# Adding the attention bias on VectorE and subtracting the maximum on GpSimd

## The reference

```
tokens  = patches(x, 16 long, step 8) @ W + b             # 64 x 93 x 128
h = tokens
xn = layernorm(layernorm(h)) * gamma + beta
q, k, v = conv3(wq1 @ xn), conv3(wk1 @ xn), conv3(wv1 @ xn)   # 8 heads of 64
sim = q k^T / 8 - |i - j| * slope_h                       # 93 x 93 for each head
sim = where(j > i, -max, sim)
h = h + (softmax(sim) @ v) @ wout^T
h = h + experts(layernorm(h))   # top 2 of 16, each expert's mean hidden row
```

## Time and profile before

| what | value |
|---|---|
| median of 3 runs | 845.18 us (844.15 to 845.42) |
| the profiled execution: its own time | 846.1 us |
| the profiled execution: its span | 844.4 us |
| PE busy | 752.6 us (89%) |
| DVE busy | 615.9 us (73%) |
| ACT busy | 468.9 us (56%) |
| POOL busy | 383.3 us (45%) |

### The profile page before, as it was taken

The page is one execution under the profiler, slowest core; times in us unless marked ns, Lnnn a source line. Parts: engine busy times, 40 slices in busy tenths (PEclk is TensorE's granted clock), DMA queues, the critical chain, the costliest instruction groups (busy, mean ns, idle before and its releaser), DMA issues. The chain is left out here.

```text
span 844.4 us, 20971 instructions
## 1 busy us (share of the span) xinstructions
PE 752.6 (89%) x6670; PEld 696.4 (82%) x6670; DVE 615.9 (73%) x1621; ACT 468.9 (56%) x1021; POOL 383.3 (45%) x408
## 2 busy tenths in 40 slices
PE   5577999999999999999999999999786318999987
PEld 5466999999999999999999999977675208999983
DVE  2145778888888888888888888899573145888865
ACT  3345566656566665656666566555333107899950
POOL 3442243666556565555656556545241552222200
PEclk9787999999999999999999999999898658999989
DMA  6321123332112112111212211050000022222205
GB/s 190 99 72 46 47 72 117 102 104 64 48 47 66 47 47 65 50 46 46 68 46 50 65 48 48 19 208 20 10 15 6 19 69 73 64 62 62 62 17 145
DMA packets 42246, 53.89 MB, mean 64 GB/s; under 512 B 13651, under 2 KB 28947, under 8 KB 41680
## 3 DMA queue, kind: packets, MB, share of 16 engines
q1 hardware_dynamic: 26304, 37.13, 15.5%
q0 software_dynamic: 13120, 14.05, 6.0%
q10 hardware_dynamic: 2768, 2.00, 0.8%
HBM read 42.69 MB, written 10.26 MB: 63 GB/s over the span
## 5 line engine op out<-in xcount | busy, mean ns | idle before, releaser
L1106 POOL DMA_INDIRECT expert_rows<-hn,slot x128 | 167.7, 1310 | 92.5 <-DVE slot L951 59.9
L1043 POOL TENSOR_TENSOR x_lo<-x_raw,x_hi 128x752 fp32r<-128x752 f32 x64 | 114.9, 1795 | 151.7 <-ACT x_hi L667 151.7
L831 DVE SCALAR_TENSOR_TENSOR qkv<-ps,taps,qkv 128x368 f32<-128x368 f32 x192 | 114.0, 594 | 86.2 <-ACT qkv L675 84.6
L675 ACT ACTIVATE qkv<-ps,taps 128x372 f32<-128x372 f32 x192 | 108.6, 567 | 90.1 <-PE ps L408 89.8
L834 DVE SCALAR_TENSOR_TENSOR qkv<-ps,taps,qkv 128x364 f32<-128x364 f32 x192 | 114.6, 597 | 6.8
L406 PE MATMUL ps<-x_hi,wtok_hi 128*128 128x376 f32 x256 | 95.3, 372 | 11.3 <-DVE wtok_lo L811 9.0
L500 PEld LDWEIGHTS psO<-vrow,probT 93*93 93x93 f32 x1024 | 93.5, 162 | 4.7 <-ACT probT L700 3.2
L500 PE MATMUL psO<-vrow,probT 93*93 93x65 f32 x1024 | 93.9, 245 | 2.0 <-ACT probT L700 1.1
L407 PE MATMUL ps<-x_lo,wtok_hi 128*128 128x376 f32 x256 | 89.1, 348 | 0.0
L408 PE MATMUL ps<-x_hi,wtok_lo 128*128 128x376 f32 x256 | 89.0, 348 | 0.0
L576 PE MATMUL psO<-wout,attnT 128*93 128x128 f32 x512 | 70.6, 283 | 18.6 <-ACT attnT L746 15.8
(11 more groups left out here) (160 smaller groups left out, 1620.7 us busy)
## 6 DMA issues: line engine op xcount, KB each, us to landing
x_raw<-in_x SPq DMA_DIRECT2D x64, 376.0 KB, 3.2
w1s<-in_w POOLq DMA_DIRECT2D x8, 512.0 KB, 4.9
w<-in_w SPq DMA_DIRECT2D x4, 1024.0 KB, 10.3
xs<-expert_rows SPq DMA_DIRECT2D x54, 64.0 KB, 1.8
xs<-expert_rows POOLq DMA_DIRECT2D x54, 64.0 KB, 2.1
out<-resid SPq DMA_DIRECT2D x16, 160.0 KB, 2.4
expert_rows<-hn,slot POOLq DMA_INDIRECT x128, 3.5
qkv<-in_w_tok ACTq DMA_DIRECT2D x4, 256.0 KB, 6.7
```

The costliest lines, as they stand in the source:

```text
L675: nc.scalar.activation(qkv[u][:, k, :, :], psP[(k + 1) % 2][:, 0:GT].rearrange("p (b n) -> p b n", n=NT), ACT.Copy, scale=taps[:, k, 2:3]) ...
L831: nc.vector.scalar_tensor_tensor(dst[:, :, 1:NT], src[:, :, 0:NT - 1], taps[:, k, 1:2], dst[:, :, 1:NT], ALU.mult, ALU.add).then_inc(tap1_ ...
L1043: nc.gpsimd.tensor_tensor(x_lo[u][:, 0:PIECE], x_raw[u][:, :], x_hi[u][:, 0:PIECE].bitcast(F32), ALU.subtract)\
L1106: nc.gpsimd.indirect_dma_start(rows, bass.IndirectOffsetOnAxis(slot[1 - u][:, c:c + 1], 0), hn[1 - u][:, c % GB, :], None)\
```

## The change

`bias` stays in fp32 and goes straight from HBM to its own tile; `ident16` and the two casts are gone. TensorE no longer writes the bias into `psS`. VectorE adds `bias` as it takes the scores out of `psS` into one of two `score` tiles, and takes the maximum from there. GpSimd subtracts the maximum in place. TensorE's transposes read `score`.

```diff
-        bias = sb("bias", [NT, 2, GT], BF16)
-        ident16 = sb("ident16", [128, 128], BF16)
+        bias = sb("bias", [NT, 2, GT])
-        shifted = sb("shifted", [NT, 2, 4, NT])
+        score = [sb(f"score{u}", [NT, 2, 4, NT]) for u in range(2)]
...
@@ tensor, step
-                                mm = nc.tensor.transpose(psS[:NT, a, hh * NT:(hh + 1) * NT], shifted[:, a, hh, :],
+                                mm = nc.tensor.transpose(psS[:NT, a, hh * NT:(hh + 1) * NT], score[(s + 1) % 2][:, a, hh, :],
...
                         wait(pe, p_evac, n * 2)
-                        for a in range(2):
-                            nc.tensor.matmul(psS[:NT, a, 0:4 * NT], ident16[:NT, :NT], bias[:, a, :],
-                                             start=True, stop=False, skip_group_check=True)
+                        wait(pe, mask_add, n)
...
-                                                      start=False, stop=True, skip_group_check=True)
+                                                      start=True, stop=True)
@@ vector, step
                         dve.wait_ge(s_mm, n + 1)
-                        nc.vector.tensor_reduce(rmax[:, :, :], heads(psS, NT), AXX, ALU.max).then_inc(max_done, 1)
-                        dve.wait_ge(max_done, n + 1)
-                        wait(dve, p_tr, n * 2)
-                        nc.vector.tensor_tensor(shifted[:, :, :, :], heads(psS, NT),
-                                                rmax[:, :, :].unsqueeze(3).broadcast_to([NT, 2, 4, NT]),
-                                                ALU.subtract).then_inc(shift_done, 1)
+                        wait(dve, p_tr, (n - 1) * 2)
+                        nc.vector.tensor_tensor(score[s % 2][:, :, :, :], heads(psS, NT),
+                                                bias[:, :, :].rearrange("p a (h n) -> p a h n", n=NT),
+                                                ALU.add).then_inc(mask_add, 1)
+                        dve.wait_ge(mask_add, n + 1)
+                        wait(dve, shift_done, n)
+                        nc.vector.tensor_reduce(rmax[:, :, :], score[s % 2][:, :, :, :], AXX, ALU.max).then_inc(max_done, 1)
@@ gpsimd, constants
-                nc.gpsimd.tensor_copy(bias[:, :, :].rearrange("p a n -> p (a n)"), bias32[:, :]).then_inc(bias_cast, 1)
-                nc.gpsimd.tensor_copy(ident16[:, :], ident[:, :]).then_inc(bias_cast, 1)
@@ gpsimd, step, behind xnT_lo and ahead of the spread scatters
+                    if f.attn:
+                        pool.wait_ge(max_done, n + 1)
+                        nc.gpsimd.tensor_tensor(score[s % 2][:, :, :, :], score[s % 2][:, :, :, :],
+                                                rmax[:, :, :].unsqueeze(3).broadcast_to([NT, 2, 4, NT]),
+                                                ALU.subtract).then_inc(shift_done, 1)
```

More of the change, by code:

```diff
@@ L98, in build @@
         early = qkv[1][:].rearrange("p k b n -> p (k b n)")
-        bias32, tri32 = early[:NT, 0:2 * GT], early[:NT, 2 * GT:2 * GT + NT]
+        tri32 = early[:NT, 0:NT]
         early0 = qkv[0][:].rearrange("p k b n -> p (k b n)")
@@ L217, in build @@
             sem("proj_mm"), sem("tap2_done"), sem("tap1_done"), sem("conv_done"))
-        v_tr, v_evac, s_mm, max_done, shift_done = (
-            sem("v_tr"), sem("v_evac"), sem("s_mm"), sem("max_done"), sem("shift_done"))
+        v_tr, v_evac, s_mm, mask_add, max_done, shift_done = (
+            sem("v_tr"), sem("v_evac"), sem("s_mm"), sem("mask_add"), sem("max_done"), sem("shift_done"))
         p_tr, p_evac, pv_mm, den_done, norm_done = (
@@ L383, in _ @@
                 sp.dma_start(dst, src).then_inc(proj_w_in, 16)
-            for dst, src in ((bias32[:, :], c_bias), (tri32[:, :], c_tri)):
+            for dst, src in ((bias[:, :, :].rearrange("p a n -> p (a n)"), c_bias), (tri32[:, :], c_tri)):
                 sp.dma_start(dst, src).then_inc(mask_in, 16)
@@ L512, in step @@
                         if s == 0 and isinstance(t, int) and t == 3:
-                            pe.wait_ge(bias_cast, 4)
+                            pe.wait_ge(bias_cast, 2)
                         wait(pe, p_evac, n * 2)
-                        for a in range(2):
-                            nc.tensor.matmul(psS[:NT, a, 0:4 * NT], ident16[:NT, :NT], bias[:, a, :],
-                                             start=True, stop=False, skip_group_check=True)
+                        wait(pe, mask_add, n)
                         for hh in range(4):
@@ L874, in step @@
                     if f.attn:
+                        if s == 0 and isinstance(t, int) and t == 3:
+                            dve.wait_ge(mask_in, 16 * 2)
                         dve.wait_ge(s_mm, n + 1)
-                        nc.vector.tensor_reduce(rmax[:, :, :], heads(psS, NT), AXX, ALU.max).then_inc(max_done, 1)
-                        dve.wait_ge(max_done, n + 1)
-                        wait(dve, p_tr, n * 2)
-                        nc.vector.tensor_tensor(shifted[:, :, :, :], heads(psS, NT),
-                                                rmax[:, :, :].unsqueeze(3).broadcast_to([NT, 2, 4, NT]),
-                                                ALU.subtract).then_inc(shift_done, 1)
+                        wait(dve, p_tr, (n - 1) * 2)
[5 more added lines that the diff above has]
+                        nc.vector.tensor_reduce(rmax[:, :, :], score[s % 2][:, :, :, :], AXX, ALU.max).then_inc(max_done, 1)
                     if f.gate and s == 3:
@@ L1059, in step @@
                 for s in range(GB):
+                    n = (t - 3) * GB + s
                     if f.scat and not f.norm and s == 0:
```

## The result

| | before | changed |
|---|---|---|
| median of 4 runs | 845.08 us | 871.25 us (870.39 to 872.05) |
| ratio | | 1.0311, 95% interval 1.0293 to 1.0329 |
| span of the profiled execution | 844.4 us | 870.0 us |

The changed kernel is 3.1% slower. The forecast of 877 us has the sign right, and the time lies in its range. The parts of the sum are another matter: four of them came out too large, and 8.3 us have a cause that no part of it named.

A forecast was written before the change was run, and what follows sets the result against it. TensorE's instruction list was taken to bound the main stretch, and cross-engine chains the phase's end. Terms 14.0+1.6+3.6+6.0-0.3+5.3+1.4 = +31.6 us on the 844.4 us span gave 876.0, adjusted to 877 us; range 858 to 899.

The forecast's parts named there:

- s=2: Third batch part of a four-batch group: TensorE's list of 9.15 us outlasts the chain, so -0.41 us.
- the next T comes 4.0 us after the add's start: Add, maximum, GpSimd subtract and three handoffs take 4.0 us until T, the start of TensorE's softmax-dependent transpose (line 452).
- step 16: Emptying pipeline, group step without token work: nothing hides the chain, 36.0 against 32.35 us, +3.6 us.
- +1.08: Net change in us per full group of four batches, over thirteen groups (steps 3 to 15): +14.0 us.
- s=1: Second batch part of a group: chain of 8.65 us against TensorE's list of 8.14, +0.10 us.
- s=3: Last batch part of a group: GpSimd's subtract stands behind its 752- and 372-element subtracts, +1.39 us.
- s=0: First batch part of a group: chain of 9.3 us against TensorE's list of 8.89, no change.
- rival C: Handoffs and VectorE's slack better than read: adds in s=1 and s=0 start 0.4 us earlier; 866 us, chance 0.18.
- Steps 17 and 18: Pipeline's end: eight scatters ahead of GpSimd's subtract delay transposes; first +6.0 and -0.3 us, then +5.3 and +1.4.
- Rival A: GpSimd is quick: its subtract costs 0.81 us like the cast, kernel faster at 842 us; chance 0.06.
- D: Rival: a broadcast operand makes GpSimd's subtract cost up to 2.6 us; 920 us, chance 0.05.
- B: Rival: TensorE's pauses before every s=0 bring 3 us at half clock per group; +20, 897 us, chance 0.13.

The follow-up runs named there:

- e4: Changed kernel with GpSimd subtracting the full 93x744 bias table instead of the broadcast maximum, which is left out of the scores; 882.97 us.
- e8: Changed kernel without VectorE's extra wait before the maximum, and in part 3 GpSimd's subtract of the maximum ahead of the 372-element low half; 857.86 us.
- e3: Changed kernel with the eight scatters of steps 17 and 18 behind GpSimd's subtract instead of ahead of it; 868.88 us.
- e10: Changed kernel without VectorE's extra wait, and with the scatters of steps 17 and 18 spread two to a part behind the subtract; 844.28 us.
- e5: Kernel before with eleven small VectorE memsets ahead of the loop and one already fulfilled wait per batch, giving the changed kernel's code layout; 856.75 us.
- e1: Changed kernel without VectorE's wait, ahead of each maximum, for the subtract of the batch before; 864.36 us.
- e7: Changed kernel without VectorE's extra wait, and with every subtract of the maximum on VectorE instead of GpSimd; 862.27 us.
- e2: Kernel before with one already fulfilled VectorE wait per batch added, no memsets; 844.31 us.
- e9: Changed kernel without VectorE's extra wait, subtract ahead of the 372-element low half in part 3, scatters of steps 17 and 18 spread two to a part; 838.6 us.

## Why the prediction was right, and where it was not

**Direction and bounds.** The forecast was that the saving on TensorE's list is real but the chain gets longer by more. The rows bear this out, with a smaller saving than its 0.41 us a batch: in s=2, which waits for nothing, the list is 0.31 shorter, because the score products now start 0.09 later than the bias products did (T+3.83, before T+3.74). And TensorE idles 40 us ahead of L451.

**The chain, "the next T comes 4.0 us after the add's start".** Over-sized. At the end of step 16 the subtract starts at 590.11 and the T behind it is at 591.59; the add is at 588.15, so the chain takes 3.44 us. Of the 0.56 between, 0.35 are the subtract and 0.2 the handoffs, which I took at 0.12 each. Step 16 shows it: parts of 8.51, 8.40, 8.19 and 8.37 instead of three of 8.9 and one of 9.3, +1.1 instead of +3.6. The first batch was to come 1.6 later and came 0.3 earlier, within what the first T differs from profile to profile.

**The subtract, "I take 1.78".** The row of the same operation was the right one to scale (e4: 1.77) and the wrong one to read: its second operand is full. Bounds of 0.81 and 2.6 held the 1.43. The Trainium skill's "GPSIMD Engine Reference", section "Elementwise — side-by-side cycle accounting", had given an estimate of 1.63 us, scaled from its figure for 2048 elements; the trace has less, and the measurement decides.

**A group, "+1.08".** Without a pause it is +0.16: s=1 -0.05 (forecast +0.10; no wait for the subtract there, but TensorE's projection with `wout`, line 573, starts 0.2 late behind ScalarE's `attnT`), s=2 -0.31 (-0.41), s=3 +0.93 (+1.39), s=0 -0.42 (0). The mechanism in s=3 is as described: the low halves end at T+8.70 (forecast 8.73), the subtract at T+10.09 (10.5), and TensorE has GpSimd as its releaser. e8 confirms it from the other side. s=0 is where rival C was right: the add starts at T+5.09 (forecast 5.3) and the chain behind it takes some 3.4 us, so that TensorE's own list of 8.88 wins. Thirteen groups at +1.08 were the largest term of the sum, and it is the one that failed: +1.8 us in place of +14.0.

**Steps 17 and 18, "+6.0, -0.3" and "+5.3, +1.4".** The block of scatters ahead of the subtract was read right: T+17.26 and T+16.54, against T+17.7 and T+16.5. e3 moves the wait with the block and e10 removes it: T to T is then 8.5 and 7.5 us. The last term failed: the last two batches of step 18 take 18.7 us (10.64 and 8.04) where I put 2x8.1, since the clock stays at half until about 675 us, a good 20 us. I had priced half clock from the 3 us of the earlier trace rows.

**What the sum lacked.** The forecast said of steady groups that they take 37.7 us. Those of steps 6 to 13 take 36.78 or, three of them, 39.5, because VectorE stands still at the branch back. e5 shows this in the kernel before, e1 shows the changed kernel without it. That the pause is a load of instructions is read from the queue's packets, 2 or 3 at each pause. The prediction treated code as free. In favour of the mechanism the Trainium skill's "Runtime: NRT & Kernel Launch", section "Instruction fetch mechanics", says that an engine holds two pages of 256 instructions, and that a taken branch to a target outside them makes the engine wait for a fetch. The traces agree in kind: pauses with the loop at 299 to 562 and 300 to 563, none at 288 to 543, 288 to 551 and 291 to 548. Whether the start or the end of the loop decides, and where the edge lies (starts 291 and 299, ends 551 and 562), no run shows.

By the sum of its terms the prediction thus missed one cause of +8.3 and one of +3.3 (the clock in step 18), and over-read the chain by 17.6 us; that it landed only 6 us above the measured time is in good part luck, because these cancel. The emptying pipeline came nearest: steps 16 to 18 were to add 16.0 us and added 15.8, though there too step 16 was put 2.5 us too high and step 18 3.3 too low. Without the pauses the changed kernel takes 864.36 us (e1), next to the 866 of rival C, and C's reasons, adds that start earlier and shorter handoffs, are part of why; the cheaper subtract is the other part. Rival A (subtract of 0.81 us) and D (2.6) are refuted by the 1.43; B (half clock in the main stretch) by the clock of 1.00 from 110 to 560 us. B was nearer than this says: in e5 and e7 TensorE's clock did fall in the main stretch, behind waits of 1.8 to 2.1 us.

## To carry to other kernels

Before an operation is moved off a busy engine, write down what stands ahead of it on the engine that receives it, at the ends of the pipeline too: there eight scatters of 1.6 us each stood ahead of an operation of 1.4 us. Price an operation by a row with the same kinds of operands, not only the same operation and size. When an engine idles with no releaser at a place that recurs once per pass of its loop, look at the instruction queue's packets, and at where the loop lies in that engine's code, before arguing about data.

## What the runs showed of the hardware that I had not expected

- **The place of a loop in an engine's code.** Eleven instructions ahead of it and one a batch in it cost the kernel before 12.5 us (e5), a part of it by TensorE's clock, with 37 packets instead of 22 on the instruction queue; the one a batch alone costs nothing (e2).
- **A broadcast operand is cheaper on GpSimd**: 1.43 against 1.77 us for 93x744 elements (changed kernel and e4).
- **A tiny cast can be held for a whole instruction of the other engine.** The cast of 93x8 at L951 takes 0.16 us in steps 17 and 18, and 1.79 where GpSimd's 752-element subtract began 0.03 us before it; both end at 339.8. It is so behind all three pauses (1.79, 1.79 and 1.76 us, each ending 0.02 to 0.03 us behind GpSimd's instruction). The Trainium skill's "SBUF — State Buffer", section "Who interferes with whom", has casts among the operations that can need the port pair which VectorE shares with GpSimd, and lets the one that issues first hold it for its whole instruction; the rows agree.
- **The clock fell and came back unevenly.** In the changed kernel it stood at 0.50 from about 652 to 672 us although TensorE was busy 3.97 of 4 us at 656 and 4.00 of 4 at 664. In the kernel before it was back at 1.00 some 6 us after the wait that ends at 600.26. The kernel before, busy times by stretch there, columns as in the earlier trace rows:

```profile
603.00:606.00 3.00, 3.00 (x21) 2.99 (x19) 0.00 (x0) 2.23 (x5) 0.00 (x0) 0.60 0.00 0
606.00:612.00 6.00, 6.00 (x67) 5.58 (x67) 5.43 (x10) 2.14 (x5) 0.00 (x0) 1.00 0.01 3
```

It also fell behind very different waits: in e5 behind two of three waits of 2.1 us, in e7 behind two of three of 1.76, in e1 behind one of 1.72, in e9 behind none of 1 us or more. What makes the difference no run settled.
